# A graph network on one core: 16 dense chunks moved into the first mean pass, which keeps fewer PSUM banks, and a third pass that rectifies and scans in PSUM

## The reference, cut to what matters

```python
def _sage_conv(x, src, dst, Wl, bl, Wr):
    msg = x[src]
    summed = jax.ops.segment_sum(msg, dst, num_segments=N_NODES)
    cnt = jax.ops.segment_sum(jnp.ones((src.shape[0],), x.dtype), dst, num_segments=N_NODES)
    mean = summed / jnp.maximum(cnt, 1.0)[:, None]
    return mean @ Wl.T + bl + x @ Wr.T
...
h = relu(_sage_conv(x, src, dst, Wl0, bl0, Wr0))
h = relu(_sage_conv(h, src, dst, Wl1, bl1, Wr1))
h = _sage_conv(h, src, dst, Wl2, bl2, Wr2)
x = _layernorm(x + h)
...
x = _layernorm(x + attention(x, edge_attr_128, src, dst))
```

## Time and profile before

| | |
|---|---|
| median of three runs | 2648.06 us (2647.51 to 2650.15) |
| profiled execution, its own time | 2644.61 us |
| its span in the profile | 2642.8 us |
| TensorE busy | 1873.9 us, 71% |
| TensorE weight loads | 1316.8 us, 50% |
| VectorE busy | 1729.4 us, 65% |
| ScalarE busy | 1095.2 us, 41% |
| GpSimd busy | 1770.9 us, 67% |
| granted TensorE clock, mean | 0.854 of full speed |

### The profile page before, as it was taken

The page is one execution under the profiler, slowest core; times in us unless marked ns, Lnnn a source line. Parts: engine busy times, 40 slices in busy tenths (PEclk is TensorE's granted clock), DMA queues, the critical chain, the costliest instruction groups (busy, mean ns, idle before and its releaser), DMA issues.

```text
span 2642.8 us, 43434 instructions
## 1 busy us (share of the span) xinstructions
PE 1873.9 (71%) x10441; PEld 1316.8 (50%) x10441; DVE 1729.4 (65%) x5671; ACT 1095.2 (41%) x2508; POOL 1770.9 (67%) x1895
## 2 busy tenths in 40 slices
PE   4755666999989999677777673888788877770000
PEld 2324565666656666455555453555555555540000
DVE  7787886777767777565555533888888878881000
ACT  7951111544534444122222222777666666650000
POOL 0046776566756676467777777777777777766776
PEclk7558999999999999788888885999999999995555
DMA  0025666788877887545445623455445445433321
GB/s 19 1 56 148 165 159 138 174 195 189 177 172 187 189 192 173 154 125 135 126 128 142 164 68 106 144 158 157 144 143 152 145 140 152 140 104 104 94 92 51
DMA packets 366730, 357.03 MB, mean 135 GB/s; under 512 B 46534, under 2 KB 288724, under 8 KB 366584
## 3 DMA queue, kind: packets, MB, share of 16 engines
q1 hardware_dynamic: 310136, 246.40, 31.0%
q0 software_dynamic: 56448, 109.10, 20.3%
HBM read 232.83 MB, written 129.11 MB: 137 GB/s over the span
## 4 chain that ended last, share of the span: by engine, by line
PE 32%; POOL 26%; issue 17%; DVE 13%; DMA 5%; ACT 5%; POOLq 1%; DVEq 0%; SPq 0%; ACTq 0%
POOL GX L675 10%; POOL hsrc L675 9%; PE bank L852 9%; PE bank L872 5%; POOL out_dram L729 4%; PE bank L774 3%; PE bank L900 3%; PE bank L892 3%; PE bank L890 3%; DMA GX<-in_x_dram,idx_a 3%; PE bank L856 2%; ACT normed L1021 2%; ACT normed L1022 2%; DVE stats L1358 2%; POOL x_prime L729 2%
## 5 line engine op out<-in xcount | busy, mean ns | idle before, releaser
L675 POOL DMA_INDIRECT GX<-mean_product,idx_a x392 | 411.2, 1049 | 129.5 <-issue 113.9
L675 POOL DMA_INDIRECT GX<-in_x_dram,idx_a x392 | 378.1, 965 | 117.9 <-issue 108.9
L852 PE MATMUL bank<-h,wt 128*128 128x512 f32 x588 | 321.0, 657 | 0.1
L1046 ACT ACTIVATE logv<-mv,eps 128x4 f32<-128x4 f32 x245 | 72.2, 295 | 541.5 <-DVE mv L1363 541.4
L729 POOL DMA_INDIRECT x_prime<-normed,idx_b x196 | 197.6, 1008 | 88.0 <-issue 83.4
L729 POOL DMA_INDIRECT out_dram<-XN,idx_b x196 | 192.8, 984 | 76.0 <-issue 64.8
L675 POOL DMA_INDIRECT hsrc<-x_prime,idx_d x196 | 189.7, 968 | 59.7 <-issue 59.7
L675 POOL DMA_INDIRECT GX<-in_edge_attr_dram,idx_a x196 | 189.7, 968 | 58.6 <-issue 53.5
L675 POOL DMA_INDIRECT hsrc<-x_prime,idx_c x196 | 186.7, 953 | 59.7 <-issue 59.7
L774 PE MATMUL bank<-ident,GX 128*128 128x128 f32 x588 | 104.5, 307 | 155.5 <-DMA GX<-in_x_dram,idx_a 149.5
L774 PE MATMUL bank<-ident,hsrc 128*128 128x128 f32 x468 | 86.5, 316 | 119.0 <-DMA hsrc<-x_prime,idx_d 57.4
(11 more groups left out here) (231 smaller groups left out, 4656.0 us busy)
## 6 DMA issues: line engine op xcount, KB each, us to landing
mean_product<-prod SPq DMA_DIRECT2D x147, 256.0 KB, 4.3
hsrc<-mean_product SPq DMA_DIRECT2D x147, 256.0 KB, 4.4
XN<-in_x_dram SPq DMA_DIRECT2D x98, 256.0 KB, 4.5
x_prime<-normed SPq DMA_DIRECT2D x98, 256.0 KB
XN<-x_prime SPq DMA_DIRECT2D x98, 256.0 KB, 4.5
out_dram<-normed SPq DMA_DIRECT2D x98, 256.0 KB
flag<-same_dst_row SPq DMA_DIRECT2D x147, 128.0 KB, 4.3
XN<-low_row SPq DMA_DIRECT2D x98, 128.0 KB
```

What stands on the lines that cost most here:

```text
L675: pool.indirect_dma_start(buf[:, c.slot(U), t, :], None, table, bass.IndirectOffsetOnAxis(ap=idx[:, c.slot(U), t:t + 1], axis=0)).then_inc ...
L852: last = pe.matmul(psum[:, :], wt[:, T_R[i], :], before[:, c.slot(2), :], start=True, stop=not dst_phase)
```

## The change

Three things are changed together.

1. The dense chunks are divided 16, 41 and 41 (`BEFORE`, `EACH`) over the three passes instead of 0, 49 and 49. In `mean0` they run through `zeroth`, which marks them `narrow`. For them all leads of the edge work in `mean0` rise by `TABLE` = 5, and the table is made at step -6 (`at`).
2. The banks of `mean0` are laid out anew: the turned chunk has bank 5 alone, the products bank 3 alone, the look-up banks 4 and 7 alone, the narrow dense chunks banks 0, 1, 2 and, for `chain_y`, 6. Events that had to be two chunks old must now be one chunk old. `hot` is single, in `dst` too. `XN` is free for node rows, and masks, picked rows and table lie elsewhere.
3. In `mean2` ScalarE rectifies in bank 5 and the scan reads it there; `hsrc` is not written. `mean_turn` of the next chunk waits for the scan too.

```diff
+BEFORE = 16
+TABLE = 5
...
-def run(eng, phase, stages, count, to_end=True, middle=None):
+def run(eng, phase, stages, count, to_end=True, middle=None, at=0):
...
+        if middle and s == -at:
+            middle()
         single(s)
-    if middle:
-        middle()
-    with eng.Fori(0, whole) as j:
-        for u in range(U):
-            for lead, f, _ in stages:
-                f(At(phase, j, u + lead))
+    if whole:
+        with eng.Fori(0, whole) as j:
+            for u in range(U):
+                for lead, f, _ in stages:
+                    f(At(phase, j, u + lead))
...
+    EACH = (NN - BEFORE) // 2
...
-        low_all = spare([2, CH], BF16)
-        hot = spare([2, 2, CH], BF16)
-        picked = spare([TPC, WIDE], BF16)
...
+        low_all = sb("low_all", [P, 2, CH], BF16)
...
+        hot = res[:, 2, :, :].rearrange("p t d -> p (t d)").bitcast(BF16).rearrange("p (a n) -> p a n", a=2)
...
-        def turn_bank(c):
-
-            return (5, 2)[c.slot(2)]
+        def prod_bank(c):
+
+            return bank[3] if c.phase == "mean0" else bank[3 + c.slot(2)]
+
+        def y_bank(c):
+
+            return bank[6] if c.narrow else bank[6 + c.slot(2)]
...
+        def zeroth(f):
+
+            def of(c):
+                one = At("dense", c.j, c.u)
+                one.narrow = True
+                f(one)
+            return of
+
         def first(f):
 
-            return lambda c: f(At("dense", c.j, c.u))
+            return lambda c: f(At("dense", c.j, c.u + BEFORE))
 
         def second(f):
 
-            return lambda c: f(c.later("dense", NC))
+            return lambda c: f(c.later("dense", BEFORE + EACH))
...
-            run(sp, "mean0", [(LAG + 3, flag_load), (2, low_load), (LAG, prod_store)], NC)
-            look_done.end(sp, "mean0")
-            run(sp, "mean1", [(6, flag_load), (DENSE + 8, first(x_load)), (1, prod_store), (DENSE, first(x_store))], NC)
-            run(sp, "mean2", [(6, flag_load), (DENSE + 8, second(x_load)), (1, prod_store), (DENSE, second(x_store))], NC)
+            run(sp, "mean0", [(TABLE + LAG + 3, flag_load), (TABLE + 2, low_load), (TABLE + LAG, prod_store),
+                              (8, zeroth(x_load), BEFORE), (0, zeroth(x_store), BEFORE)], NC)
+            run(sp, "mean1", [(6, flag_load), (DENSE + 8, first(x_load), EACH), (1, prod_store), (DENSE, first(x_store), EACH)], NC)
...
-                pe.wait_ge(added.of(c), added.free(c))
-                y = bank[6 + c.slot(2)]
+                pe.wait_ge(added.of(c), added.after(c, 1 if c.narrow else 2))
+                y = y_bank(c)
...
-                if c.phase == "mean0":
-                    pe.wait_ge(m_h.of(c), m_h.after(c, 2))
-                    pe.wait_ge(m_seg.of(c), m_seg.after(c, 2))
-                    psum = bank[turn_bank(c)]
-                else:
-                    pe.wait_ge(m_h.of(c), m_h.after(c, 1))
-                    psum = bank[5]
+                pe.wait_ge(m_h.of(c), m_h.after(c, 1))
+                if c.phase != "mean1":
+                    pe.wait_ge(m_seg.of(c), m_seg.after(c, 1))
+                psum = bank[5]
...
-                pe.wait_ge(m_scaled.of(c), m_scaled.free(c))
+                pe.wait_ge(m_scaled.of(c), m_scaled.after(c, 1 if c.phase == "mean0" else 2))
...
-                return ((0, 1), (6, 7))[c.slot(2)] if c.phase == "mean0" else (3, 4)
+                return (4, 7) if c.phase == "mean0" else (3, 4)
...
-                pe.wait_ge(look_done.of(c), look_done.after(c, 2 if c.phase == "mean0" else 1))
+                pe.wait_ge(look_done.of(c), look_done.after(c, 1))
...
-                    run(pe, "mean0", [(LAG + 1, mean_turn), (0, look_up), (LAG, mean_prod)], NC, middle=table_sums)
+                    run(pe, "mean0", [(TABLE + LAG + 1, mean_turn), (TABLE, look_up), (TABLE + LAG, mean_prod),
+                                       (4, zeroth(chain_t), BEFORE), (3, zeroth(chain_1), BEFORE),
+                                       (2, zeroth(chain_2), BEFORE), (1, zeroth(chain_y), BEFORE)], NC,
+                        middle=table_sums, at=TABLE + 1)
                     look_done.end(pe, "mean0")
+                    before = At("dense", 0, BEFORE - 1)
+                    pe.wait_ge(added.of(before), added.after(before))
...
-                    act.activation(h, bank[5][:, :], ACT.Relu, bias=bcol[:, i - 1:i]).then_inc(m_h.of(c), 1)
+                    act.activation(h if i == 1 else bank[5][:, :], bank[5][:, :], ACT.Relu, bias=bcol[:, i - 1:i]).then_inc(m_h.of(c), 1)
...
-                    run(act, "mean0", [(0, mean_keep)], NC)
+                    run(act, "mean0", [(TABLE + LAG + 1, mean_keep), (4, zeroth(keep_t), BEFORE), (3, zeroth(keep_1), BEFORE),
+                                        (2, zeroth(keep_2), BEFORE), (1, zeroth(inverse_root), BEFORE)], NC)
...
-                    rows = take_cols(hsrc, c.index() * CH, CH)
+                    rows = take_cols(hsrc, c.index() * CH, CH) if c.phase == "mean1" else bank[5][:, :]
...
-                dve.wait_ge(look_sum.of(c), look_sum.after(c, 2))
+                dve.wait_ge(look_sum.of(c), look_sum.after(c, 1))
...
-                    run(dve, "mean0", [(LAG + 1, mean_seg), (LAG, mean_scale), (1, look_hot_rows), (0, look_take)], NC,
-                        middle=make_table)
+                    run(dve, "mean0", [(TABLE + LAG + 1, mean_seg), (TABLE + LAG, mean_scale), (TABLE + 1, look_hot_rows),
+                                        (TABLE, look_take), (1, zeroth(add_x), BEFORE), (0, zeroth(norm), BEFORE)], NC,
+                        middle=make_table, at=TABLE + 1)
```

More of the change, by code:

```diff
@@ L47 @@
 class At:
+    narrow = False
     def __init__(self, phase, j, u, last=False, per=U):
@@ L397, in gnn_kernel @@
         m_prod = signal("m_prod", 2, 1, MEANS)
-        m_scaled = signal("m_scaled", 2, 1, MEANS)
+        m_scaled = signal("m_scaled", 1, 1, MEANS)
         m_stored = signal("m_stored", 4, 16, MEANS)
@@ L897, in mean_prod @@
                 pe.wait_ge(m_seg.of(c), m_seg.after(c))
-                pe.wait_ge(m_scaled.of(c), m_scaled.free(c))
+                pe.wait_ge(m_scaled.of(c), m_scaled.after(c, 1 if c.phase == "mean0" else 2))
                 for t in range(TPC):
-                    last = pe.matmul(bank[3 + c.slot(2)][:, t * P:(t + 1) * P], seg[:, c.slot(2), t * P:(t + 1) * P],
+                    last = pe.matmul(prod_bank(c)[:, t * P:(t + 1) * P], seg[:, c.slot(2), t * P:(t + 1) * P],
                                      wt[:, T_L[int(c.phase[-1])], :], start=True, stop=True)
@@ L914, in look_banks @@
             def look_banks(c):
-                return ((0, 1), (6, 7))[c.slot(2)] if c.phase == "mean0" else (3, 4)
+                return (4, 7) if c.phase == "mean0" else (3, 4)
             def look_up(c):
                 pe.wait_ge(look_hot.of(c), look_hot.after(c))
-                pe.wait_ge(look_done.of(c), look_done.after(c, 2 if c.phase == "mean0" else 1))
+                pe.wait_ge(look_done.of(c), look_done.after(c, 1))
                 if c.phase == "mean0":
-                    pairs = [(hot[:, c.slot(2), a, :], node_table[:, a, b, :]) for a in range(2) for b in range(2)]
+                    pairs = [(hot[:, a, :], node_table[:, a, b, :]) for a in range(2) for b in range(2)]
                 else:
-                    pairs = [(hot[:, c.slot(2), 0, :], dst_table[:, b, :]) for b in range(2)]
+                    pairs = [(hot[:, 0, :], dst_table[:, b, :]) for b in range(2)]
                 width = COLS if c.phase == "mean0" else WIDE
@@ L1340, in add @@
                 s = c.slot(2)
-                y = by_tile(bank[6 + c.slot(2)][:, :])
+                y = by_tile(y_bank(c)[:, :])
                 dve.wait_ge(y_done.of(c), y_done.after(c))
@@ L1387, in mean_seg @@
                     dve.wait_ge(m_turned.of(c), m_turned.after(c))
-                    rows = bank[turn_bank(c)][:, :]
+                    rows = bank[5][:, :]
                 else:
                     dve.wait_ge(m_h.of(c), m_h.after(c))
-                    rows = take_cols(hsrc, c.index() * CH, CH)
+                    rows = take_cols(hsrc, c.index() * CH, CH) if c.phase == "mean1" else bank[5][:, :]
                 dve.wait_ge(flag_in.of(c), flag_in.after(c))
@@ L1402, in mean_scale @@
                 inv = take_cols(col_f[:, 1, :], c.index() * TPC, TPC).rearrange("p (t a) -> p t a", a=1).to_broadcast([P, TPC, D])
-                dve.tensor_tensor(prod[:, c.slot(4), :, :], by_tile(bank[3 + c.slot(2)][:, :]), inv, ALU.mult)\
+                dve.tensor_tensor(prod[:, c.slot(4), :, :], by_tile(prod_bank(c)[:, :]), inv, ALU.mult)\
                    .then_inc(m_scaled.of(c), 1)
@@ L1437, in look_hot_rows @@
                 dve.wait_ge(low_in.of(c), low_in.after(c))
-                dve.wait_ge(look_sum.of(c), look_sum.after(c, 2))
+                dve.wait_ge(look_sum.of(c), look_sum.after(c, 1))
                 for a in range(2 if c.phase == "mean0" else 1):
```

(4 more changed lines are left out.)

36 lines of the change are left out of this document (13 added, 23 removed).

## The result

The changed kernel takes 2739.32 us (median of 6 runs, 2733.96 to 2746.45), the kernel before 2648.57 us in the same comparison (6 runs, 2646.49 to 2652.07). The ratio is 1.0342, 95% interval 1.0327 to 1.0358: 91 us slower, where 39 were forecast and 2720 was the upper end of the range. The profiled execution has a span of 2737.9 us (+95.1), and TensorE's mean granted clock fell from 0.854 to 0.841.

The account below looks back on a forecast made before the run. VectorE was taken as fullest in the first pass, TensorE as the limit in the second and third. The trace terms summed to +27.1 us, with the clock +38.8: 2683.4 profiled, about 2687 median, range 2658 to 2720.

Parts of the forecast that it names:

- Term 3: First pass, light steps: each look-up waits for the previous take, 5.43 us a step, 135.8 us for 25 steps.
- Term 4: First pass, 16 dense steps: VectorE sets the pace at 7.2 us a step, 115.2 us in all.
- Term 7: TensorE's clock in the first pass and its tail, taken as 0.91: +11.7 us, bounds 0 and +60.8.
- first rival: First pass: single banks cost nothing, light steps at VectorE's 4.10 us; total -17.3, 2631 us; chance 0.06.
- Term 5: Ends of the first pass: -2 us ahead of the table, +8.7 us behind the last turn.
- second rival: First pass: TensorE's clock falls as in `dst`, up to 2736 us; chance 0.14 for a time above 2708.
- Term 1: Second pass: eight steps fall from 6.21 to 2.86 us, 26.8 less; 11.7 if the gathers' lead fails.
- Term 2: Third pass: 26.8 us less, but 12.1 more from the new wait in about ten light steps; net -14.7.
- third rival: Third pass hides its new wait, clock stays at 1.00: +15.0, 2663 us; chance 0.12 for 2653 to 2669.
- Term 6: `dst`: with single `hot`, a 0.35 us mask stands between look-up and take; +3 us, 0 to +5.

Follow-up runs that it names:

- e8: Changed kernel with look-up, turned-chunk and product banks and masks double again in the first pass once its 16 dense chunks are through: 2669.48 us, ratio 1.0079.
- e2: Changed kernel with two idle TensorE matmuls per step of the first pass from look-up 23 on, in steps without dense work: 2707.27 us, ratio 1.0228.
- e3: Changed kernel with GpSimd copying gather indices two chunks at a time right ahead of their gather, not four at a time one chunk ahead: 2730.66 us, ratio 1.0311.
- e6: Kernel before with only the third pass changed (rectifier in bank 5, scan reads it there, next turn waits for the scan): 2651.33 us, ratio 1.0011.
- e4: Changed kernel with the third pass as before (rectifier writes `hsrc`, turn waits for the rectifier alone): 2736.24 us, ratio 1.0347.
- e1: Changed kernel with dense chunks divided 0, 49 and 49 as before, keeping the bank layout, leads and third pass: 2750.67 us, ratio 1.0394.
- e5: Kernel before with every look-up of the first pass on one pair of banks, all else as before: 2746.05 us, ratio 1.0366.

## Why the prediction was right or wrong

**What bounds the kernel.** "So moving a dense chunk ... into the first loads VectorE, the engine with least room there" was half right. In the kernel before the step of 4.75 us was the gathers' (34.6 us of waiting in 30 turns), and VectorE's own 4.10 showed only where gathers were ahead (e8: 4.08). VectorE's room was the 0.65 us between them.

**Term 3, the light steps: the round right, its clock wrong.** 5.43 us was forecast at full clock and 5.50 measured in e2, and in the two short steps of the changed kernel itself. In the changed kernel the 20 steps from 369.83 to 507.33 take 6.88 each.

**Term 4, the dense steps: right.** 7.11 us in the mean over 15 steps (258.11 to 364.81) against 7.2. Three slips of the working move nothing: TensorE's turn, look-up and product add up to 2.71 us there, not 2.86; the excess of Term 7 is 2.27, not 2.28; and the first rival's end comes to -2.2, not -2.4.

**Term 5, the ends: right in kind, too low.** The round of the tail was given 3.9 us; the look-ups after the change start at 521.10, 526.49, 531.09, 536.51, 541.06 and 546.37, 5.05 us apart in the mean, three of the six 2.77 long. +18.0 instead of +10.1, and e2 with its full clock has +9.6 (55.3 - 45.7): the term without its clock was good to about a microsecond.

**Term 7, the clock: the step that failed first.** "I take the 0.91, as TensorE keeps about half its time busy, nearer to that row than to the other." The row of 0.91 was from a stretch where look-ups ran ahead in their second pair of banks. The row of 0.53 had been described, in the same part, as the one "where TensorE did the same alternation with VectorE", and that alternation is what single banks make. The clock came out at 0.76 in the light steps and 0.74 in the tail, that is, 48 and 52% of the time at 1.2 GHz instead of 18%. The reason given does not fit the rows either: TensorE was busy 67% of the row of 0.91 (13.42 of 20.00 us) and 51% of that of 0.53 (17.30 of 34.00), so "about half" was the other row's. And the clock costs more than a mean over the window says: 48% of 2.27 us would be 1.09 a step, but the low stretches fall on the look-up. In the 20 light steps it takes 2.57 us in the mean and the product 1.45, against 1.52 and 1.08 in e2, together 1.42 more, which is the 6.88 - 5.50 = 1.38 us of the step to within 0.04. Forecast were 0.41, so 8 us in these 20 steps, and it was 28.

The Trainium skill, TensorE: Matmul & The Clock Gate, section A second HAM failure mode, had said that cycling banks with small idle times between makes the clock go back and forth. By that rule, the prediction had written, the pass "would come out nearer to the upper bound", and the trace agrees: look-ups of 1.52 and of 2.77 us stand in the same tail. It agrees on the idle times, not on the cycling: e8 goes through two pairs of banks in turn and has a clock of 1.00 where the single pair has 0.76.

**The second rival** ("up to ... 2736"), given 0.14, had this cause, and the median lies 3 us above its figure. That nearness is luck. Its 2736 needs 60.8 us of clock; the clock cost some 36 here (27.5 in the light steps, 8.4 in the tail by the difference of the gaps, 63.7 - 55.3), and the missing 25 us are about those that the second and third pass failed to give.

**Term 1, the second pass: the other step that failed.** "The gathers have eight chunks of room ... so their lead covers these steps." -8.5 instead of -26.8. The room is 4 to 7 chunks by the way the indices are copied, and GpSimd adds a chunk only every 5.0 us, so the lead lasts for three light steps. With e3's order eight steps stay at 2.86, and the pass gains 11 us more. The other value that the term had worked out, 11.7 at the gathers' pace, was the nearer one; it had taken 4.75 where GpSimd's queue shows 5.0.

**Term 2, the third pass.** -8.4 instead of -14.7, for the same reason: light steps of 4.14 as forecast (4.07), and two late gathers (steps of 6.14 and 7.17). That the full steps hide the wait is shown by e6. The third rival was wrong on the clock, and on this pass its premise did not count: the wait stands open in the light steps, but without it the pass is only 0.7 us shorter (e4), not 12.1.

**Term 6, the dst phase.** The first result in `dst` is written 2.0 us later relative to the last scan, forecast +3; the rest behind it adds 3.4, which the runs don't explain.

**The first rival**, single banks for nothing, is refuted by e1 and e5: single look-up banks alone cost 98 us (e5). In this kernel the 16 moved chunks gained 11 us by the medians (e1 2750.7, changed kernel 2739.3) and 14 by the ratios, and the layout made for them lost 103 (e1: 2750.7 - 2647.5).

## What to carry to other kernels

When a change makes two engines take turns, look for the stretch of the old trace in which they already do, and take the clock from that row, not from the stretch that is being changed. Price it by the durations of the operations on the path, not by the mean clock of a window. Before letting an operation share one PSUM bank, write down the whole round through that bank (here cast, look-up, product, scale, masks, take); every instruction in it is then on the path, and a change of TensorE's clock shows in full. Before counting on a stream's lead, work out how fast its own queue refills it and how many slots its bookkeeping really lets it run ahead.

## What the runs showed that was not expected

- Adding 1.88 us of useless matmuls to each step took 1.38 us off the step and 32 us off the kernel, while the granted clock went from 0.76 to 1.00.
- TensorE's busy share hardly shows what happened to it: 62% of 390 to 510 us after the change, 67% in the kernel before where the clock was 0.91. The wait ahead of a look-up differs more, 2.56 us after the change, 1.31 in the earlier trace rows, 0.94 in e2, but it does not settle a single look-up: the one at 411.92 waited 2.64 us and still ran in 1.52. What exactly makes the clock fall, the runs don't tell.
- With the gathers further ahead, a scan waited 7.24 us for a row of flags in the third pass of e3, and three steps took 33 us together instead of 18; in its second pass, with the same lead, nothing was late. The lead alone does not explain it.
